# Seven expert halves and a down product at other places of a hand-written scan order, and one value product ahead of a gate-network product

## The chip, the cores and the metric

One Trainium2 chip, one of its cores. The metric is the time of one execution on the device in microseconds (us), the median over repeated runs; lower is better. The core's engines work through separate instruction queues, each strictly in the order in which the kernel issues on it, and meet only through semaphores: TensorE (PE, its weight loads PEld), VectorE (DVE), ScalarE (ACT), GpSimd (POOL), and SyncE (SP), which issues most DMAs.

## What is computed

A layer of gated delta-rule attention, followed by a mixture of eight expert networks with the best two of eight per token, on 8 sequences of 256 tokens of width 128, all in float32. Cut to what matters:

```python
x = x + attention(layernorm(x))       # delta rule, 4 heads of 32, chunks of 32 tokens
x = x + experts(layernorm(x))

# attention: per sequence and head, a serial loop over 8 chunks
def step(S, inp):
    qi, ki, ui, wi = inp
    attn = jnp.where(tri_s, 0.0, qi @ jnp.swapaxes(ki, -1, -2))
    u_i = ui - wi @ S
    o = qi @ S + attn @ u_i
    S = S + jnp.swapaxes(ki, -1, -2) @ u_i
    return (S, o)
# four paths (two convolutions, delta, v) are mixed by weights of a small gate network
# that reads mean and variance of each path ("stats")

# experts
gate_scores = jax.nn.softmax(x @ Wg); topk_scores, topk_idx = jax.lax.top_k(gate_scores, 2)
gate  = jnp.einsum('bsh,ehi->bsei', x, W11)
value = jnp.einsum('bsh,ehi->bsei', x, W12)
fused = gate * jax.nn.sigmoid(gate) * value
expert_out = jnp.einsum('bsei,eih->bseh', fused, W2)   # then the weighted sum of two experts
```

## The kernel before

The 8 sequences are worked as four pairs of 512 tokens. One software pipeline runs over the pairs: a call of `body(u, t, b, c)` projects and normalises pair u, runs the delta rule's serial chunk loop for pair t, the experts for pair b and what is left of the experts of pair c. Five calls cover everything: b is none, 0, 1, 2, 3. The last (`ALONE`) has only experts. In the first there are none. So the serial loop and the experts stand side by side in three calls. Here they are called **scan 1, 2 and 3** (experts of pair 0, 1 and 2) and **tail 1, 2 and 3** (what follows each scan in the same call). Scan 3 has no pair u left: no scores, no masks, no beta.

All experts are computed for all tokens. An expert has 256 inner columns in two **halves** i (half i belongs to expert i // 2), and a half is four steps: `gate` (PE, three matmuls of 128x512: high part, low part of the weights, low part of the input), `sig` (ACT, silu of the gate product into `sg`, in the trace `toep_room`), `value` (PE, three such matmuls), `fuse` (DVE, their product into `fu`, in the trace `v_room`). `y` is the down product of an expert (PE, L585) and needs both its halves; `add` (DVE, four instructions, L1197) weights it by the router and adds it up. `weigh` (DVE, 20 instructions, L1150 to L1175) computes those weights, and `add` needs it; `y` does not.

The chunk loop has eight chunks n. PE computes **u(n)** into ps4, ACT copies it to `u_sb` (L945), PE computes **s(n)** into ps3 and o(n) into ps2 (L441), ACT copies s to `s_sb` (L953), and u(n+1) needs that copy. Between these fixed links stand the lists of `SCAN`: `SCAN[2n]` behind u(n), `SCAN[2n+1]` behind s(n) and o(n). Each engine runs only its own steps of a list, in the list's order:

```python
run(SCAN[2 * n])          # L723 on PE, L947 on ACT
...                       # s(n), o(n)
run(SCAN[2 * n + 1])      # L742 on PE, L955 on ACT
```

On DVE the lists simply follow one another. Other steps that the text names: `norms` (DVE, and behind it the pow on POOL, L362), `norm` (DVE, normalised keys and queries, L1048 to L1057; it sets `kq_ready`), `g` 0 and 1 (PE, scores, ps0 and ps1, need `kq_ready`), `mask` (DVE, L1065 to L1075, needs both g and sets `attn_ready`), `centre` (DVE, L1229 to L1232), `square` (ACT, L850), `spread` (DVE), `stats` (DVE, transposes the statistics), `hidden_s` (PE, L614, the gate network's product over the statistics, needs `stats_ready`), `hidden_x` (PE, L606), `router` (PE, DVE, and an exp on ACT, which loads another activation table, L917), `beta`/`tanh`/`beta_hc` (PE, ACT, DVE).

PSUM banks: gate products go to ps5 and value products to ps6 while a single bank is used for each (`bank_of` gives 0), so a gate product waits for the `sig` of the half before, and a value product for the `fuse` of the half before. Where `two_banks` is true, odd halves use ps0 and ps1, which the scores leave free only once `attn_ready` is set. For pairs 2 and 3 two banks are used throughout.

Of the kernel before, what the change touches and what calls it, by code (L numbers as in the profile page):

```python
# [28 lines left out]
E, FF = 8, 256  # L29
FC = FF // P  # L30
# [26 lines left out]
def dgv(i):  # L57
    return [(what, i) for what in ("dgate", "dsig", "dvalue")]
# [6 lines left out]
         ("dfuse", 13)]  # L65
SCAN = [[("ln_cen", 1), ("ln_sq", 1), ("dy", 6), *dgv(14), ("dadd", 6), ("ln_var", 1), ("conv", 3)],
        [("dfuse", 14), *dgv(15), ("ln_out", 1), ("dfuse", 15)], [("x2t", 1), ("dy", 7), ("dadd", 7)],
        [("q_silu", 0), ("q_hc", 0), ("qk_sq", 0), ("norms", 0)],
        [("router", 1), ("beta", 0), ("tanh", 0), ("beta_hc", 0), ("dstore", 0)],
        [("gate", 0), ("sig", 0), ("value", 0), ("fuse", 0)],  # L70
        [("gate", 1), ("sig", 1), ("value", 1), ("fuse", 1), ("norm", 0), ("gate", 2)],
        [("sig", 2), ("value", 2), ("gate", 3), ("fuse", 2)], [("g", 0), ("weigh", 0)], [("g", 1), ("mask", 0)],
        [("sig", 3), ("value", 3), ("fuse", 3), ("centre", 0), ("square", 0)],
        [("y", 0), ("add", 0), ("centre", 3), ("spread", 0)], [("gate", 4), ("sig", 4), ("value", 4), ("fuse", 4)],
        [("gate", 5), ("square", 3), ("sig", 5), ("value", 5), ("spread", 3)], [("fuse", 5)],
        [("gate", 6), ("centre", 1), ("sig", 6), ("value", 6), ("square", 1)]]
TAIL = [("delta", 0), ("fuse", 6), ("centre", 2), ("spread", 1), ("square", 2), ("y", 1), ("gate", 7), ("sig", 7),
        ("value", 7), ("hidden_x", 0), ("spread", 2), ("fuse", 7), ("stats", 0), ("gate", 8), ("sig", 8),
        ("gelu_set", 0), ("hidden_s", 0), ("add", 1), ("value", 8), ("y", 2), ("gelu", 0), ("exp_set", 0), ("fuse", 8),
        ("logits", 0), ("add", 2), ("y", 3), ("gate", 9), ("exp_in", 0), ("exp", 0), ("sig", 9), ("value", 9),  # L80
        ("softmax", 0), ("fuse", 9), ("add", 3)]

# [21 lines left out]
def build(nc, x, early, taps_row, late, toep_in, w11, w12, w2, out):  # L104
    ctx = ExitStack()
    with ctx:
        def sb(name, *shape):
            return ctx.enter_context(nc.sbuf_tensor(name, [P, *shape], F32))
# [306 lines left out]

        def two_banks(p, i):

            return p >= 2 or 4 <= i < (10, E * FC)[p]

        def bank_of(p, i):  # L420
            return i % 2 if two_banks(p, i) else 0
# [14 lines left out]
        def _(pe):  # L436
# [112 lines left out]
            def body(u, t, b, c):  # L549
# [905 lines left out]
```

## Time and profile before

| | us |
|---|---|
| median of 3 runs | 429.35 |
| lowest and highest | 425.93, 431.18 |
| the profiled execution, whole | 426.13 |
| its span, first to last instruction | 424.4 |
| PE busy | 344.0 |
| DVE busy | 276.2 |
| ACT busy | 146.2 |
| POOL busy | 90.2 |

The profiled execution lies 3.2 us below the median; 1.7 us of it lie outside of its span. The mean granted clock of TensorE in it is 0.918 of full speed. A busy time is no path: the engines wait for one another in turn, and what ends a wait has to be looked up in the timeline.

### The profile page before, as it was taken

To read this page: it belongs to the slowest core of one execution; us is meant where nothing else is said; L and a number is where in the kernel's file an instruction comes from. 1 tells how busy PE (TensorE), PEld (TensorE's weight loads), DVE (VectorE), ACT (ScalarE), POOL (GpSimd) and SP (SyncE) were. 2 spreads that over 40 slices of the span, in tenths; PEclk is the share of its full clock that TensorE was granted. 3 is DMA by queue.
4 is the path that set the end of the run, shared out by engine and by line. 5 is a ranking of instruction groups with operands and counts; after the bars stand their busy time and mean duration, and the time that the engine had idled before them with its cause. 6 is when DMAs were issued, how large, how long until landed. Compare 5 with 4: busy or idle time off the path is not lost.

```text
span 424.4 us, 14279 instructions
## 1 busy us (share of the span) xinstructions
PE 344.0 (81%) x6364; PEld 253.7 (60%) x6364; DVE 276.2 (65%) x639; ACT 146.2 (34%) x264; POOL 90.2 (21%) x152
## 2 busy tenths in 40 slices
PE   7988977954657796888988869899897987867996
PEld 6344963643324565655776557477675755755885
DVE  3788931268747569767755797498739659667554
ACT  1342613301434351453413413533252353133221
POOL 4862000051622061440200715202000000200000
PEclk9699888968598779999999899899989899899999
DMA  7331350005120001110000011200000000000000
GB/s 255 124 94 29 40 123 19 5 3 129 15 37 4 3 2 28 15 25 14 5 2 2 26 29 15 38 3 3 2 28 4 2 0 0 2 25 2 0 2 25
DMA packets 42652, 12.47 MB, mean 29 GB/s; under 512 B 35424, under 2 KB 41696, under 8 KB 42464
## 3 DMA queue, kind: packets, MB, share of 16 engines
q1 hardware_dynamic: 39440, 9.47, 10.4%
q10 hardware_dynamic: 3152, 2.10, 1.6%
q8 instruction: 50, 0.82, 0.8%
q14 instruction: 10, 0.08, 0.1%
HBM read 8.68 MB, written 2.88 MB: 27 GB/s over the span
## 4 chain that ended last, share of the span: by engine, by line
PE 53%; DVE 24%; issue 8%; DMA 6%; ACT 4%; POOL 4%; SPq 0%; DVEq 0%; ACTq 0%
PE ps L546 17%; PE ps L585 12%; PE ps L441 9%; PE ps L485 7%; PE ps L471 3%; DVE x L1197 2%; DVE v_room L1186 2%; PE ps L614 2%; DMA a_d<-a_hc 2%; DMA t<-t_d 1%; DMA t_d<-t_it 1%; POOL t_it L386 1%; DVE toep_room L1230 1%; PE ps L633 1%; POOL rn L362 1%
## 5 line engine op out<-in xcount | busy, mean ns | idle before, releaser
L1186 DVE TENSOR_TENSOR v_room<-toep_room,ps 128x512 f32<-128x512 f32 x64 | 43.7, 684 | 44.1 <-PE ps L546 20.2
L585 PE MATMUL ps<-w_sb,v_room 128*128 128x128 f32 x512 | 64.9, 281 | 8.9 <-DVE x L1197 4.5
L585 PEld LDWEIGHTS ps<-w_sb,v_room 128*128 128x128 f32 x512 | 62.4, 195 | 14.3 <-issue 8.2
L546 PE MATMUL ps<-x_hi,w_sb 128*128 128x512 f32 x128 | 61.7, 482 | 4.0 <-DVE v_room L1186 2.6
L830 ACT ACTIVATE toep_room<-ps 128x512 f32<-128x512 f32 x64 | 38.1, 597 | 60.1 <-PE ps L546 56.6
L546 PE MATMUL ps<-x_lo,w_sb 128*128 128x512 f32 x128 | 52.4, 409 | 0.0
L546 PE MATMUL ps<-x_hi,w_lo 128*128 128x512 f32 x128 | 52.3, 409 | 0.0
L1197 DVE SCALAR_TENSOR_TENSOR x<-ps,rs,x 128x128 f32<-128x128 f32 x128 | 35.8, 342 | 16.5 <-PE ps L585 16.5
L362 POOL TENSOR_TENSOR rn<-ss,mh 128x16 f32<-128x16 f32 x8 | 23.1, 2901 | 65.1 <-DVE ss L1037 65.1
L396 POOL TENSOR_TENSOR g<-gm,mh 128x16 f32<-128x16 f32 x4 | 11.6, 2909 | 112.2 <-DVE gm L1298 112.2
L546 PEld LDWEIGHTS ps<-x_hi,w_sb 128*128 128x128 f32 x128 | 25.3, 198 | 13.3 <-DVE v_room L1186 3.6
L546 PEld LDWEIGHTS ps<-x_hi,w_lo 128*128 128x128 f32 x128 | 25.7, 201 | 5.4 <-issue 2.2
L546 PEld LDWEIGHTS ps<-x_lo,w_sb 128*128 128x128 f32 x128 | 25.1, 196 | 6.0
L441 PEld LDWEIGHTS ps<-u_sb,taps_room 32*32 32x32 f32 x960 | 17.2, 115 | 14.2 <-issue 14.0
L441 PE MATMUL ps<-v_hc,toep_room 32*32 32x64 f32 x768 | 23.8, 281 | 1.5 <-DVE v_hc L1012 1.5
L441 PE MATMUL ps<-u_sb,taps_room 32*32 32x32 f32 x960 | 20.6, 203 | 4.8 <-issue 4.2
L441 PEld LDWEIGHTS ps<-v_hc,toep_room 32*32 32x32 f32 x768 | 20.5, 123 | 3.8 <-DVE v_hc L1012 2.3
L485 PE MATMUL ps<-xnp,wkc 128*128 128x512 f32 x32 | 19.8, 758 | 1.7 <-DVE v_room L1186 1.0
L441 PE MATMUL ps<-vb,t_t 32*32 32x32 f32 x512 | 13.0, 200 | 9.4 <-ACT s_sb L953 9.4
L441 PEld LDWEIGHTS ps<-vb,t_t 32*32 32x32 f32 x512 | 10.0, 110 | 17.0 <-issue 16.4
L850 ACT ACTIVATE psq<-toep_room 128x512 f32<-128x512 f32 x16 | 10.0, 626 | 28.1 <-DVE toep_room L1230 28.1
L945 ACT ACTIVATE u_sb<-ps 128x64 f32<-128x64 f32 x32 | 7.2, 225 | 33.9 <-PE ps L441 33.9
(199 smaller groups left out, 595.7 us busy)
## 6 DMA issues: line engine op xcount, KB each, us to landing
toep_room<-in_toep SPq DMA_DIRECT2D x1, 1536.0 KB, 12.1
a_d<-a_hc SPq DMA_DIRECT2D x4, 256.0 KB, 3.6
t<-t_d SPq DMA_DIRECT2D x4, 256.0 KB, 3.0
v_room<-in_w SPq DMA_DIRECT2D x1, 1024.0 KB, 6.4
v_room<-in_w ACTq DMA_DIRECT2D x1, 1024.0 KB, 6.6
out_y<-x ACTq DMA_DIRECT2D x4, 256.0 KB, 2.3
taps_room<-in_taps SPq DMA_DIRECT2D x1, 768.0 KB, 5.7
x_sb<-in_x SPq DMA_DIRECT2D x1, 768.0 KB, 8.9
```

Source lines behind the costliest of these rows:

```text
L362: pool.tensor_tensor(rn[:, a, :], ss[:, a, :], mh[:, 0:M], ALU.pow).then_inc(s["rn_ready"], 1)
L396: pool.tensor_tensor(g1[:, :], gm[:, :], mh[:, 0:M], ALU.pow).then_inc(s["orn_ready"], 1)
L441: ins = pe.matmul(bank[q, col:col + n], lhs(q), rhs(q), skip_group_check=True, **kw)
L471: ins = pe.matmul(ps[4 + i][:, :], wvc[:, k, :], xnp[:, 2 * i:2 * i + 2, k:k + L], start=(k == 0), stop=(k == 3))
L485: ins = pe.matmul(ps[bank][:, :], w[:, k, :], xnp[:, bass.ds(u * 2, 2), k:k + L], start=(k == 0), stop=(k == 3))
L546: ins = pe.matmul(bank[:, :], a[cols].bitcast(F32R), c[:, :].bitcast(F32R), start=(k == 0), stop=(k == 2))
L585: ins = pe.matmul(yb[:, P * j:P * j + P], fu[:, e % 2, f, P * j:P * j + P], w2_sb[:, FC * e + f, :], start=(f == 0), stop=(f == FC - 1))
L614: pe.matmul(ps[2 + k][:, :], w1s[:, P * k:P * k + P], stats_t[:, :, :].rearrange("p m t -> p (m t)"), start=False, stop=True).then_inc(s[" ...
L830: act.activation(sg[:, i % 2, :], ps[GATE[bank_of(p, i)]][:, :], ACT.Silu).then_inc(s["sg_ready"], 1)
L850: act.activation(psq[:, p, :, :], pcen[:, p, :, :], ACT.Square).then_inc(s["psq_ready"], 1)
L1186: dve.tensor_tensor(fu[:, e % 2, f, :], sg[:, i % 2, :], ps[VALUE[bank_of(p, i)]][:, :], ALU.mult).then_inc(s["fu_ready"], 1)
L1197: ins = dve.scalar_tensor_tensor(x1[:, j, :], ps[out_bank(p, e)][:, P * j:P * j + P], rs[:, j, e:e + 1], x1[:, j, :], ALU.mult, ALU.add)
```

## The change

The steps of the first halves are moved forward in the scan, and one value product in the tail; no instruction is added or removed. In the scan, the first half starts behind s(1) and the router's product comes behind it; halves 0 to 4 and the down product of expert 0 are issued on PE before the second score product's list ends, where halves 0 to 2 and the gate of half 3 stood before. The list `SCAN[12]` is left without steps. With half 4 ahead of the masks, its gate product stays in ps5 and no longer waits for `attn_ready`; half 5 does now. `add` 0, `weigh`, `mask` and the centre and square steps keep their order among each other.

```diff
-        [("q_silu", 0), ("q_hc", 0), ("qk_sq", 0), ("norms", 0)],
-        [("router", 1), ("beta", 0), ("tanh", 0), ("beta_hc", 0), ("dstore", 0)],
-        [("gate", 0), ("sig", 0), ("value", 0), ("fuse", 0)],
-        [("gate", 1), ("sig", 1), ("value", 1), ("fuse", 1), ("norm", 0), ("gate", 2)],
-        [("sig", 2), ("value", 2), ("gate", 3), ("fuse", 2)], [("g", 0), ("weigh", 0)], [("g", 1), ("mask", 0)],
-        [("sig", 3), ("value", 3), ("fuse", 3), ("centre", 0), ("square", 0)],
-        [("y", 0), ("add", 0), ("centre", 3), ("spread", 0)], [("gate", 4), ("sig", 4), ("value", 4), ("fuse", 4)],
+        [("q_silu", 0), ("gate", 0), ("q_hc", 0), ("qk_sq", 0), ("value", 0), ("sig", 0), ("norms", 0)],
+        [("router", 1), ("gate", 1), ("fuse", 0), ("beta", 0), ("tanh", 0), ("beta_hc", 0), ("dstore", 0)],
+        [("sig", 1), ("value", 1), ("gate", 2), ("fuse", 1), ("sig", 2)],
+        [("value", 2), ("fuse", 2), ("norm", 0), ("gate", 3), ("sig", 3)],
+        [("y", 0), ("value", 3)], [("g", 0), ("gate", 4), ("fuse", 3), ("sig", 4), ("weigh", 0)],
+        [("g", 1), ("value", 4), ("mask", 0)], [("fuse", 4), ("centre", 0), ("square", 0)],
+        [("add", 0), ("centre", 3), ("spread", 0)], [],
...
-            return p >= 2 or 4 <= i < (10, E * FC)[p]
+            return p >= 2 or 5 <= i < (10, E * FC)[p]
```

In `TAIL`, `("value", 8)` now stands ahead of `("hidden_s", 0)`; before, it stood behind `("add", 1)`.

PE in scan 1, around the fifth and sixth link of the chunk loop. ps4 is u, ps3 is s, ps5 and ps6 are gate and value products, ps7 is the down product. Before, from u(6) backwards to o(5) and on to half 4:

```order
L441 MATMUL ps2<-u_sb,taps_room 32x32 x4
L585 MATMUL ps7<-w2_sb,v_room 128x128 x8
L441 MATMUL ps4<-vb,t32_t 32x32 x4
L441 MATMUL ps4<-s_sb,wneg_t 32x32 x4
L441 MATMUL ps4<-vb,t32_t 32x32 x4
L441 MATMUL ps4<-s_sb,wneg_t 32x32 x4
L546 MATMUL ps5<-x2_hi,w11_sb 128x512
L546 MATMUL ps5<-x2_hi,w11_lo 128x512
L546 MATMUL ps5<-x2_lo,w11_sb 128x512
L546 MATMUL ps6<-x2_hi,w12_sb 128x512
L546 MATMUL ps6<-x2_hi,w12_lo 128x512
L546 MATMUL ps6<-x2_lo,w12_sb 128x512
```

Now, from the same o(5) to s(6) and o(6):

```order
L441 MATMUL ps2<-u_sb,taps_room 32x32 x4
L441 MATMUL ps4<-vb,t32_t 32x32 x4
L441 MATMUL ps4<-s_sb,wneg_t 32x32 x4
L441 MATMUL ps4<-vb,t32_t 32x32 x4
L441 MATMUL ps4<-s_sb,wneg_t 32x32 x4
L441 MATMUL ps3<-u_sb,taps_room 32x32 x8
L441 MATMUL ps2<-s_sb,taps_room 32x32 x4
L441 MATMUL ps2<-u_sb,taps_room 32x32 x4
L441 MATMUL ps2<-s_sb,taps_room 32x32 x4
L441 MATMUL ps2<-u_sb,taps_room 32x32 x4
```

The down product in front of u(6) and the six matmuls of half 4 behind it stand further up now, so that o(5), u(6) and s(6) follow each other with nothing between.

ACT in scan 1, from the silu of the queries to the link u(3). Before:

```order
L785 ACTIVATE qf<-ps0 128x512
L789 ACTIVATE qk_sq<-qk_hc 128x1024
L945 ACTIVATE u_sb<-ps4 128x64
L917 ACT_TABLE_LOAD
L917 ACTIVATE rt<-rs 128x32
L798 ACTIVATE tb<-ps1 128x512
L953 ACTIVATE s_sb<-ps3 128x64
L830 ACT_TABLE_LOAD
L830 ACTIVATE toep_room<-ps5 128x512
L945 ACTIVATE u_sb<-ps4 128x64
```

Now:

```order
L785 ACTIVATE qf<-ps0 128x512
L789 ACTIVATE qk_sq<-qk_hc 128x1024
L830 ACTIVATE toep_room<-ps5 128x512
L945 ACTIVATE u_sb<-ps4 128x64
L917 ACT_TABLE_LOAD
L917 ACTIVATE rt<-rs 128x32
L798 ACTIVATE tb<-ps1 128x512
L953 ACTIVATE s_sb<-ps3 128x64
L830 ACT_TABLE_LOAD
L830 ACTIVATE toep_room<-ps5 128x512 x2
L945 ACTIVATE u_sb<-ps4 128x64
```

The silu of half 0 has moved ahead of the two table loads, and behind them stand two silus, of halves 1 and 2, ahead of the copy of u(3).

PE in tail 1, from the gate product of half 8 to the down product. Before:

```order
L546 MATMUL ps5<-x2_lo,w11_sb 128x512
L614 MATMUL ps2<-stats_t,late_sb 128x512
L614 MATMUL ps3<-stats_t,late_sb 128x512
L546 MATMUL ps6<-x2_hi,w12_sb 128x512
L546 MATMUL ps6<-x2_hi,w12_lo 128x512
L546 MATMUL ps6<-x2_lo,w12_sb 128x512
L585 MATMUL ps7<-w2_sb,v_room 128x128 x8
```

Now:

```order
L546 MATMUL ps5<-x2_lo,w11_sb 128x512
L546 MATMUL ps6<-x2_hi,w12_sb 128x512
L546 MATMUL ps6<-x2_hi,w12_lo 128x512
L546 MATMUL ps6<-x2_lo,w12_sb 128x512
L614 MATMUL ps2<-stats_t,late_sb 128x512
L614 MATMUL ps3<-stats_t,late_sb 128x512
L585 MATMUL ps7<-w2_sb,v_room 128x128 x8
```

The three matmuls of value product 8 have passed the two of `hidden_s`, which wait for the statistics.

## Rows read from the trace of the kernel before

**Rows 1.** The page's engine shares and the shares of its chain

```profile
PE 344.0 (81%) x6364; PEld 253.7 (60%) x6364; DVE 276.2 (65%) x639; ACT 146.2 (34%) x264; POOL 90.2 (21%) x152
...
PE 53%; DVE 24%; issue 8%; DMA 6%; ACT 4%; POOL 4%; SPq 0%; DVEq 0%; ACTq 0%
```

**Rows 2.** PE's waits over the span: who was waited for, us, times, longest

```profile
PE ps L441 <- ACT s_sb L953: 9.4, 10, 2.3
...
PE ps L614 <- DVE stats_t L1244: 5.6, 4, 1.9
```

**Rows 3.** PE's timeline, scan 2: start, length, work, idle time before and its end

```profile
237.60 0.50 PE L546 MATMUL ps<-x_hi,w_sb 128*128 128x512 f32 x1 [1.36 <-ACT toep_room L830]
...
250.83 2.05 PE L585 MATMUL ps<-w_sb,v_room 128*128 128x128 f32 x16
254.41 0.23 PE L441 MATMUL ps<-vb,t_t 32*32 32x32 f32 x5 [1.53 <-ACT s_sb L953]
...
254.79 0.50 PE L546 MATMUL ps<-x_hi,w_sb 128*128 128x512 f32 x1
...
256.39 0.33 PE L441 MATMUL ps<-u_sb,taps_room 32*32 32x32 f32 x16
...
258.53 0.26 PE L441 MATMUL ps<-vb,t_t 32*32 32x32 f32 x8
...
259.43 0.23 PE L441 MATMUL ps<-s_sb,taps_room 32*32 32x32 f32 x5 [0.45 <-ACT u_sb L945]
...
261.32 1.95 PE L585 MATMUL ps<-w_sb,v_room 128*128 128x128 f32 x16
263.02 0.47 PE L546 MATMUL ps<-x_hi,w_sb 128*128 128x512 f32 x1
```

**Rows 4.** DVE's timeline, scan 2

```profile
240.21 0.69 DVE L1048 TENSOR_TENSOR kn_next<-qk_hc,rn 128x512 f32<-128x512 f32 x1
...
244.41 0.18 DVE L1150 TENSOR_REDUCE st<-rt 128x4 f32<-128x32 f32 x1
...
249.18 0.88 DVE L1065 TENSOR_TENSOR a_hc<-ps,nbm 128x256 f32<-128x256 f32 x2
...
251.49 0.68 DVE L1186 TENSOR_TENSOR v_room<-toep_room,ps 128x512 f32<-128x512 f32 x1
```

**Rows 5.** ACT's timeline, scan 2

```profile
235.66 1.28 ACT L830 ACT_TABLE_LOAD   x1
...
254.06 0.21 ACT L953 ACTIVATE s_sb<-ps 128x64 f32<-128x64 f32 x1
```

**Rows 6.** PE's timeline, scan 1, u(6) and y 1

```profile
170.97 0.23 PE L441 MATMUL ps<-vb,t_t 32*32 32x32 f32 x5 [2.26 <-ACT s_sb L953]
...
177.88 1.95 PE L585 MATMUL ps<-w_sb,v_room 128*128 128x128 f32 x16
```

**Rows 7.** PE's timeline, scan 3, u(6) and y 1

```profile
326.12 0.23 PE L441 MATMUL ps<-vb,t_t 32*32 32x32 f32 x5 [1.91 <-ACT s_sb L953]
...
334.51 1.95 PE L585 MATMUL ps<-w_sb,v_room 128*128 128x128 f32 x16
```

**Rows 8.** PE's timeline, tail 1

```profile
185.35 1.98 PE L614 MATMUL ps<-stats_t,late_sb 128*128 128x512 f32 x4 [1.70 <-DVE stats_t L1244]
...
187.87 1.95 PE L585 MATMUL ps<-w_sb,v_room 128*128 128x128 f32 x16
```

**Rows 9.** PE's timeline, tail 2

```profile
268.96 3.19 PE L614 MATMUL ps<-stats_t,late_sb 128*128 128x512 f32 x4 [1.89 <-DVE stats_t L1244]
...
273.14 1.95 PE L585 MATMUL ps<-w_sb,v_room 128*128 128x128 f32 x16
```

**Rows 10.** Stretches: length, busy time and count of each engine, PE's granted clock, DMA

```profile
327.40:330.90 3.50, 3.50 (x56) 2.45 (x55) 2.33 (x6) 1.34 (x3) 0.00 (x0) 0.53 0.02 5
166.60:178.00 11.40, 8.70 (x195) 6.93 (x184) 10.40 (x24) 3.74 (x10) 4.02 (x9) 1.00 0.28 37
```

**Rows 11.** PE's timeline at the last large wait

```profile
387.01 0.50 PE L546 MATMUL ps<-x_hi,w_sb 128*128 128x512 f32 x1 [2.62 <-DVE v_room L1186]
```

More of the change, by code:

```diff
@@ L78 @@
         ("value", 7), ("hidden_x", 0), ("spread", 2), ("fuse", 7), ("stats", 0), ("gate", 8), ("sig", 8),
-        ("gelu_set", 0), ("hidden_s", 0), ("add", 1), ("value", 8), ("y", 2), ("gelu", 0), ("exp_set", 0), ("fuse", 8),
+        ("gelu_set", 0), ("value", 8), ("hidden_s", 0), ("add", 1), ("y", 2), ("gelu", 0), ("exp_set", 0), ("fuse", 8),
         ("logits", 0), ("add", 2), ("y", 3), ("gate", 9), ("exp_in", 0), ("exp", 0), ("sig", 9), ("value", 9),
```

## The prediction

> **What bounds the kernel now.** I read the page's shares first. PE is busy for 81% of the span and carries 53% of the chain that ended last, DVE 24%, ACT 4% [rows 1]. So neither engine is the bound all the time: stretches in which PE is full alternate with stretches in which it waits for DVE. The waits of PE say where. Ten waits for the copy of s by ACT, L953, make 9.4 us, and four for the statistics, L614, make 5.6 us [rows 2]. Those two kinds are what the change touches.
>
> The first kind is read in scan 2. u(6) on PE starts at 254.41 after 1.53 us idle, released by `s_sb` [rows 3]. The copy itself is short. It starts on ACT at 254.06 [rows 5], because ACT issues `square` 0 ahead of it, and that waits for `centre` 0 on DVE. DVE has no gap there: `norm` from 240.21, `weigh` from 244.41, `mask` from 249.18, `fuse` and `centre` from 251.49 [rows 4]. **So DVE's serial run from `norm` to `centre` 0 sets u(6)**, and PE's products ahead of it only have to be done by then. Behind u(6) PE is the bound until the down product y 1: 6.91 us in scan 2 (254.41 to 261.32) [rows 3] and 6.91 us in scan 1 (170.97 to 177.88) [rows 6]. In scan 3 the same work took 8.39 us (326.12 to 334.51) [rows 7], since TensorE's granted clock was 0.53 in the 3.5 us from 327.40, mostly its lower level of 1.2 GHz, against 1.00 throughout 166.6 to 178 [rows 10]. One fall of the clock there costs 8.39 - 6.91 = **1.48 us**.
>
> y 1 matters: the `fuse` of half 6 needs its buffer back, and delta's `centre`, `square`, `spread`, then `stats` follow on DVE. So a shift of y 1 passes to the whole tail.
>
> **The change part by part.** The number of instructions is equal. I go through what moves.
>
> *When u(6) comes.* The moved work does not leave DVE: between `norm` and `centre` 0 stood two `fuse`, `weigh` and `mask` (fuse 2, fuse 3), and there now stand two as well (fuse 3, fuse 4). What shifts is the start of this run.
>
> - Scan 1: `norm` now follows `fuse` 2 instead of `fuse` 1, so one gate product, one silu and one value product more are ahead of it: 0.7 + 0.6 + 0.7 = **+2.0 us**. A product is 0.7 because six matmuls and the hand-over took 1.60 (254.79 to 256.39) [rows 3]. If the products still ran at 1.2 GHz it would be 2.6 + 0.6 = 3.2; if the earlier start of half 0 is won back in full, 0.
> - Scan 2: before, PE stood 1.36 us in front of gate 1 for a silu [rows 3], which stood behind the 1.28 us table load at 235.66 [rows 5]. In the new order gate 2 waits for the silu of half 1, behind the same load. The gate product of half 1 now stands ahead of `beta` and delays `tanh` and so that load; I estimate gate 2 at 238.1, 0.5 us later than gate 1 was. Behind it come its own 0.7, u(3) 0.3, value product 2 at 0.7 and `fuse` 2 at 0.7 with hand-over, and `norm` starts near 240.6 instead of 240.21: **+0.4 us** (0 to +1.0).
> - Scan 3 has no `norm`; `weigh` follows `fuse` 3 instead of `fuse` 2, one more DVE product of 0.6 (0.68 long in [rows 4]): **+0.6 us** (0 to +0.7).
>
> *From u(6) to y 1.* Half 4, 1.60 us, stood there and covered the round trip by ACT: u(6) to s(6) took 1.98 us (254.41 to 256.39). Uncovered it takes 0.90 as from u(7) to s(7) (258.53 to 259.43, with 0.45 us idle for `u_sb`) [rows 3]. Gain 1.98 - 0.90 = 1.08, so 6.91 becomes 5.83 at full clock. y 0 ran inside the wait and costs 1.7 (261.32 to 263.02) [rows 3]; it leaves no gain, the wait only grows.
>
> *The clock.* Between the end of o(5) and u(6) PE now has nothing at all. In scan 2 y 0 stood from 250.83 and the wait was 1.53 [rows 3]; without y 0 and half 4 in reach the empty time is about 254.4 + 0.4 - 250.8 = 4.0 us, and only 0.9 us of small work and waiting follow before half 5. The trace shows no such wait in a scan. After 1.91 us idle in scan 3 the clock fell, after the 2.26 us of scan 1 it did not (1.00 in [rows 10], which holds that wait), nor after 2.62 us at 387.01, whose matmuls then start 0.34 us apart as at full speed [rows 11]. So a fall is not certain after 2 us; at 4 us I take one in each scan, at 1.48. The bounds are 0 and twice that, if half 5 and half 6 both run wholly at 1.2 GHz. The Trainium skill ("TensorE: Matmul & The Clock Gate", section "Loop structure matters more than you think") says that "whether your matmuls stay warm is determined by your loop nest" and shows a wait between matmuls as the bad case. This rule speaks against the change; by it the fall comes in every scan, as I take it; by the two rows without a fall it would come in none.
>
> Per scan, y 1 then moves by: scan 1 +2.0 - 1.08 + 1.48 = +2.4; scan 2 +0.4 - 1.08 + 1.48 = +0.8; scan 3, whose fall is in its 8.39 already, +0.6 + 5.83 + 1.48 - 8.39 = -0.5. **Scans together: +2.7 us.**
>
> *The tail.* `hidden_s` waited 1.70 us in tail 1 and 1.89 in tail 2 [rows 8, 9]. Value product 8, 0.7 us, now runs within this wait, its PSUM bank being free. From `hidden_s` to y 2 it was 187.87 - 185.35 = 2.52 us [rows 8]; two products over the statistics without the value product are 1.4 to 1.8 of it, so 0.7 to 1.1 goes, I take 0.9. y 2, fuse 8, `add` 2 and y 3 follow each other, and half 9 behind them, so the gain lasts to the end of the tail: 3 x 0.9 = **-2.7 us**. If the statistics themselves came earlier, nothing would be under the value product and its cost back at 0.7; the order on DVE gives no reason for it.
>
> In tail 2 the clock fell behind the wait: 273.14 - 268.96 = 4.18 us for what took 2.52 in tail 1 [rows 8, 9], 1.66 more. With the wait cut to 1.2 us this may be spared. I count half: **-0.8 us**.
>
> At nothing I cost three things. GpSimd's pow starts at the same time, since `norms` keeps its place on DVE. The output store on ACT comes in the same list as before. The masks' 2 us delay in scan 1 delays SyncE's chain of DMAs for the next pair, whose result is first read behind the tail; if that slack were gone, up to 2.0 us would be added, and PE would show a wait for the load of `t16`.
>
> **Sum:** +2.7 - 2.7 - 0.8 = -0.8 us. The profiled execution took 426.13, so 425.3 for one like it. The median shown is 429.35, 3.2 above it; the same step on the median gives **428.5 us**.
>
> **The rivals.**
>
> *A. The clock stays up.* For it: 2.26 and 2.62 us idle without a fall [rows 10, 11]. Then the scans give +2.0 - 1.08, +0.4 - 1.08 and +0.6 + 5.83 - 8.39, together -1.8; the tails up to -3.2, the tail's own fall -1.7: -6.7, **422.7 us**. Against it: a 4 us hole.
>
> *B. Slower: half 5 and half 6 run wholly at 1.2 GHz in all scans.* Place: the products behind s(6). Price: 2.96 instead of 1.48 per scan, +4.4; with tails at -0.7 each and no fall spared, 4.4 + 2.7 - 2.1 = +5.0, **434.4 us**. It decides as soon as the falls cost more than 1.48 + 0.8 / 3 = 1.75 us each: from there the kernel is slower than before. For it: the hole is twice any in the scans before. Against it: PE came back within 3.5 us in scan 3 [rows 10], and part of the low time lies on waits that cost nothing.
>
> *C. DVE's run isn't later at all, since half 0 two steps ahead wins scan 1 back.* Then -0.8 - 2.0 = -2.8, **426.5 us**. For it: PE has work sooner where only the router stood. Against it: the silu behind the table load stops PE either way.
>
> *D. The issue order moves something that I did not see.* Over 2% either way.
>
> **How the numbers follow.** Chances: forecast 0.42, A 0.17, B 0.18, C 0.17, D 0.06. A's and B's ends reach to 422.7 and 434.4; I leave out the last bit of B and take 422 to 434, which also holds the scatter of the runs shown (425.93 to 431.18), since it is as large as the terms. 2%, about what a measurement of this kernel can tell from no change, is 8.6 us. None of A to C reaches it, so faster and slower get only D's share and a little of A and B: 0.04 each; within 2%: 0.92.
>
> **What would show it.** In the changed profile: u(6) in scan 2 preceded by some 4 us idle on PE with `s_sb` as releaser, and DVE without a gap from `norm` to `centre` 0; s(6) 0.9 us behind u(6); a granted clock near 0.5 in the 3 us behind it; u(6) to y 1 7.3 us (5.8 if A). `hidden_s` still waits, about 1.0 to 1.2 us, with y 2 1.4 to 1.8 us behind its start. What would make the prediction wrong: idle time of PE in front of u(6) under 2.5 us, a DVE that stands idle within its run, or falls of the clock at other places than these, which two executions can differ by.

## The result, and the profile after

The changed kernel takes 434.98 us (median of 4 runs: 431.94, 434.5, 435.46, 439.89), the kernel before 427.64 beside it (4 runs, 424.03 to 431.18): **a ratio of 1.0174 [1.0104, 1.0244], slower by 1.0 to 2.4%**. Whether that is more than the 2% which the prediction took as its mark stays open. Predicted were 428.5 and a range to 434, so both are missed; of the rivals B, the slower one, lies nearest (434.4). The profiled execution is the slowest of the four, with a span of 438.1 us and a granted clock of 0.878. Here and below a ratio compares the runs of each kernel within 1.5% of its fastest, a median takes all, so the two differ by about 1% where one run lies far below the others. (The title above says seven expert halves; the scan moves five, halves 0 to 4.)

The page of the kernel after: engine shares and the shares of its chain, which answer to [rows 1].

```profile
PE 354.8 (81%) x6364; PEld 263.7 (60%) x6364; DVE 275.1 (63%) x639; ACT 146.9 (34%) x264; POOL 89.6 (20%) x152
...
PE 54%; DVE 22%; issue 9%; DMA 5%; ACT 5%; POOL 4%; SPq 0%; DVEq 0%; ACTq 0%
```

PE does the same 6364 matmuls and is busy 10.8 us longer: the same work at a lower clock. DVE's time is about the same. PE's waits, to be held against [rows 2] (us in all, times, longest):

```profile
PE ps L441 <- ACT s_sb L953: 15.2, 5, 4.5
...
PE ps L614 <- DVE stats_t L1244: 3.7, 4, 1.1
```

The wait for s, 9.4 us before, is 15.2; the wait for the statistics fell from 5.6 to 3.7, as meant. PE's timeline holds u(6) and y 1 of scans 1, 2 and 3 (against [rows 6, 3, 7]) and, in between, tail 1 (against [rows 8]):

```profile
180.15 0.33 PE L441 MATMUL ps<-vb,t_t 32*32 32x32 f32 x8 [4.44 <-ACT s_sb L953]
...
187.39 1.95 PE L585 MATMUL ps<-w_sb,v_room 128*128 128x128 f32 x16
...
194.81 1.98 PE L614 MATMUL ps<-stats_t,late_sb 128*128 128x512 f32 x4 [0.96 <-DVE stats_t L1244]
196.63 1.95 PE L585 MATMUL ps<-w_sb,v_room 128*128 128x128 f32 x16
...
265.67 0.33 PE L441 MATMUL ps<-vb,t_t 32*32 32x32 f32 x8 [4.53 <-ACT s_sb L953]
...
268.56 0.63 PE L546 MATMUL ps<-x_lo,w_sb 128*128 128x512 f32 x1
...
274.79 2.72 PE L585 MATMUL ps<-w_sb,v_room 128*128 128x128 f32 x16
...
339.13 0.41 PE L441 MATMUL ps<-vb,t_t 32*32 32x32 f32 x6 [4.25 <-ACT s_sb L953]
...
346.96 1.95 PE L585 MATMUL ps<-w_sb,v_room 128*128 128x128 f32 x16
```

The hole of some 4.0 us that was foreseen is there in every scan: 4.44, 4.53, 4.25 us. From u(6) to y 1 it then takes 7.24, 9.12 and 7.83 us, where 5.83 was the full-clock figure. The product at 268.56 shows 0.63 us, and the next one starts 0.43 behind it; at full clock they start 0.23 apart. Stretches through the hole of scan 1 (columns as in [rows 10]):

```profile
174.00:176.00 2.00, 1.22 (x81) 0.92 (x80) 1.76 (x8) 0.22 (x1) 0.00 (x0) 1.00 0.00 0
176.00:178.00 2.00, 0.00 (x0) 0.00 (x0) 1.97 (x5) 0.00 (x0) 1.27 (x1) 0.85 0.80 126
178.00:180.00 2.00, 0.00 (x0) 0.00 (x0) 1.97 (x6) 0.74 (x2) 0.00 (x0) 0.50 0.03 5
180.00:182.00 2.00, 1.43 (x80) 1.30 (x80) 1.97 (x6) 0.22 (x2) 0.00 (x0) 0.50 0.71 72
182.00:184.00 2.00, 2.00 (x12) 1.60 (x6) 1.39 (x4) 1.04 (x3) 0.19 (x1) 0.50 0.03 2
184.00:186.00 2.00, 1.55 (x68) 1.04 (x66) 1.11 (x2) 0.52 (x2) 1.61 (x6) 0.94 0.03 8
```

PE does nothing from 176 to 180. The clock falls to 0.50, its level of 1.2 GHz, while PE is idle, and stays there through u(6), s(6) and half 5, until shortly after 184.

To compare scans across executions I count from the last thing that every version does alike, the copy of `x2t` on ACT (L912) shortly ahead of the first half. In scan 1 of the kernel after it is this row, and 145.19 before:

```profile
149.98 0.60 ACT L912 ACTIVATE x2t<-ps 128x512 f32<-128x512 f32 x1 [2.49 <-PE ps L678]
```

So 4.8 of the 13.7 us between the two profiled spans have arisen before any moved instruction has run: they are scatter between executions (over all the twenty traces the row stands between 143.36 and 151.01). The scans and tails account for the next 6.9, as follows (us; in each cell scan or tail 1, 2, 3; the last line ends at the third table load behind y 1, L830):

| | before | after | difference | predicted |
|---|---|---|---|---|
| copy to u(6) | 25.78, 27.37, 21.34 | 30.17, 29.46, 22.82 | +4.39, +2.09, +1.48 | +2.0, +0.4, +0.6 |
| u(6) to y 1 | 6.91, 6.91, 8.39 | 7.24, 9.12, 7.83 | +0.33, +2.21, -0.56 | +0.40, +0.40, -1.08 |
| y 1 to the table load in the tail | 15.59, 17.43, 15.44 | 14.85, 15.79, 14.74 | -0.74, -1.64, -0.70 | -0.9, -1.7, -0.9 |

The lines add up to +7.96, +1.98 and -3.08, against +3.0, -0.3 and -3.5. (In tail 2 the last cell holds 0.8 for the clock.) The first line is the big miss. DVE's timeline shows where part of it lies, first in scan 2, then in scan 3:

```profile
253.34 0.65 DVE L1057 TENSOR_TENSOR kb<-kn_next,beta 128x512 f32<-128x512 f32 x1
255.06 0.69 DVE L1186 TENSOR_TENSOR v_room<-toep_room,ps 128x512 f32<-128x512 f32 x1 [1.07 <-issue]
...
330.81 0.69 DVE L1186 TENSOR_TENSOR v_room<-toep_room,ps 128x512 f32<-128x512 f32 x1 [3.24 <-PE ps L546]
331.42 0.18 DVE L1150 TENSOR_REDUCE st<-rt 128x4 f32<-128x32 f32 x1
```

DVE's run from `norm` to `centre` 0 has a hole now: `fuse` 3 stands idle for 1.07 us in scan 2 and for 3.24 in scan 3, and `weigh` (L1150) stands behind it. [Rows 4] have no such gap; in scan 3 before, `fuse` 2 waited 1.46 us in that place. Both times value product 3 comes late on PE. In scan 3 y 0 stands ahead of it, which is tested below. In scan 2 it is the clock: the last matmul of value product 3 starts at 254.57, and ahead of it TensorE's granted clock had fallen. The kernel after, and below it the same stretch in e0, a second profile of the same kernel:

```profile
250.21:252.21 2.00, 2.00 (x52) 1.29 (x51) 1.97 (x4) 0.64 (x2) 0.49 (x1) 0.50 0.00 0
```

```profile
250.04:252.04 2.00, 2.00 (x61) 1.91 (x61) 1.97 (x4) 0.82 (x2) 0.50 (x1) 1.00 0.00 0
```

In e0, at 1.00, `fuse` 3 doesn't wait, and u(6) of scan 2 comes 28.22 us behind the copy instead of 29.46.

### The profile page after: what moved, and what is told of

Same layout as the page of the kernel before. It is cut to its first block, busy times and chain, and to the rows that moved or that the text cites. A ratio compares the mean times of both kernels' runs of the same rounds, so it can differ in the third digit from the quotient of the medians.

```text
span 438.1 us, 14278 instructions
## 1 busy us (share of the span) xinstructions
PE 354.8 (81%) x6364; PEld 263.7 (60%) x6364; DVE 275.1 (63%) x639; ACT 146.9 (34%) x264; POOL 89.6 (20%) x152
## 4 chain that ended last, share of the span: by engine, by line
PE 54%; DVE 22%; issue 9%; DMA 5%; ACT 5%; POOL 4%; SPq 0%; DVEq 0%; ACTq 0%
PE ps L546 16%; PE ps L585 13%; PE ps L441 10%; PE ps L485 7%; PE ps L471 3%; DVE x L1197 3%; DVE v_room L1186 2%; DMA a_d<-a_hc 2%; DMA t<-t_d 1%; PE ps L614 1%; DMA t_d<-t_it 1%; ACT L830 1%; PE ps L687 1%; PE ps L633 1%; POOL t_it L386 1%
## 5 line engine op out<-in xcount | busy, mean ns | idle before, releaser
L585 PE MATMUL ps<-w_sb,v_room 128*128 128x128 f32 x512 | 67.1, 287 | 9.1 <-DVE x L1197 4.7
L585 PEld LDWEIGHTS ps<-w_sb,v_room 128*128 128x128 f32 x512 | 64.5, 201 | 15.8 <-issue 10.0
L546 PE MATMUL ps<-x_hi,w_sb 128*128 128x512 f32 x128 | 62.7, 489 | 4.8 <-ACT toep_room L830 3.1
L830 ACT ACTIVATE toep_room<-ps 128x512 f32<-128x512 f32 x64 | 38.0, 596 | 69.4 <-PE ps L546 67.5
L546 PE MATMUL ps<-x_hi,w_lo 128*128 128x512 f32 x128 | 54.8, 428 | 0.0
L546 PE MATMUL ps<-x_lo,w_sb 128*128 128x512 f32 x128 | 54.3, 424 | 0.0
L546 PEld LDWEIGHTS ps<-x_hi,w_sb 128*128 128x128 f32 x128 | 26.5, 207 | 12.9 <-ACT toep_room L830 4.1
L546 PEld LDWEIGHTS ps<-x_lo,w_sb 128*128 128x128 f32 x128 | 26.6, 208 | 6.6
L546 PEld LDWEIGHTS ps<-x_hi,w_lo 128*128 128x128 f32 x128 | 26.8, 210 | 4.7 <-issue 1.2
L441 PE MATMUL ps<-vb,t_t 32*32 32x32 f32 x512 | 13.9, 208 | 15.2 <-ACT s_sb L953 15.2
```

What stands on the lines that cost most here:

```text
L441: ins = pe.matmul(bank[q, col:col + n], lhs(q), rhs(q), skip_group_check=True, **kw)
L546: ins = pe.matmul(bank[:, :], a[cols].bitcast(F32R), c[:, :].bitcast(F32R), start=(k == 0), stop=(k == 2))
L585: ins = pe.matmul(yb[:, P * j:P * j + P], fu[:, e % 2, f, P * j:P * j + P], w2_sb[:, FC * e + f, :], start=(f == 0), stop=(f == FC - 1))
L830: act.activation(sg[:, i % 2, :], ps[GATE[bank_of(p, i)]][:, :], ACT.Silu).then_inc(s["sg_ready"], 1)
```

## The experiments

My theory after the result had two parts: the hole lets TensorE's clock fall, and that costs the time; and u(6) is late because of what now stands ahead of DVE's run. The rival for the first part: the order alone costs the time and the clock is a symptom. For the second part: only the later place of `norm` does it, or only the front (half 0 and gate 1 ahead of the router). The kernel before had medians of 428.57, 428.18, 428.18, 427.5 and 430.1 us in the five groups. All results, each ratio with its 95% interval:

| label | what it is | us, median | ratio to before |
|---|---|---|---|
| e0_after_again | the change | 432.15 | 1.0191 [1.0008, 1.0374] |
| e1_tail_only | before, tail edit alone | 423.61 | 0.9894 [0.9829, 0.9959] |
| e16_tail_again | the same | 423.78 | 0.9909 [0.9865, 0.9953] |
| e2_scan_only | the change without tail edit | 434.63 | 1.0109 [1.0016, 1.0203] |
| e3_hole_filled | the change, hole filled | 427.98 | 0.9933 [0.988, 0.9987] |
| e4_hole_work_back | the change, y 0 and half 4 back | 427.53 | 1.0035 [0.9931, 1.0139] |
| e9_y0_back | the change, only y 0 back | 432.72 | 1.0206 [1.0019, 1.0393] |
| e5_front_only | before, front alone | 427.29 | 0.9925 [0.9878, 0.9972] |
| e6_front_back | the change, front undone | 435.66 | 1.0179 [1.0113, 1.0244] |
| e7_norm_early | the change, `norm` early | 432.51 | 1.0149 [1.0068, 1.0229] |
| e11_filled_norm_early | e7, hole filled | 428.39 | 0.9912 [0.9851, 0.9974] |
| e14_value3_first | the change, value 3 ahead of y 0 | 432.84 | 1.0146 [1.0021, 1.0271] |
| e13_value3_first_filled | e14, hole filled | 426.85 | 0.9972 [0.9888, 1.0055] |
| e18_both | e7 and e14 together | 432.5 | 1.0019 [0.9975, 1.0064] |
| e17_both_filled | e18, hole filled | 426.76 | 0.9882 [0.9793, 0.997] |
| e8_front_and_tail | before, front and tail edit | 422.02 | 0.9947 [0.9908, 0.9986] |
| e15_front_tail_again | the same | 422.9 | 1.001 [0.9932, 1.0087] |
| e12_front_tail_filled | e8, hole filled | 424.41 | 0.9913 [0.9877, 0.995] |

### The two halves of the change, and the change again

e2 is the kernel after with `("value", 8)` of `TAIL` back behind `("add", 1)`; e1 and e16 are the kernel before with it moved ahead of `hidden_s`, and nothing else.

```diff
-        ("gelu_set", 0), ("hidden_s", 0), ("add", 1), ("value", 8), ("y", 2),
+        ("gelu_set", 0), ("value", 8), ("hidden_s", 0), ("add", 1), ("y", 2),
```

> The kernel before with one edit: value product 8 ahead of hidden_s in the tail. My tail term says 2.1 to 3.2 us less than before, ratio near 0.994, with the wait in front of the first L614 of each tail down from 1.7 us to about 1.0 and y 2 about 0.7 to 1.1 us sooner. The rival, that a later wait takes this back (the exp and its table load on ACT), gives a ratio of 1.000 with the interval around it.

> The changed kernel with value product 8 back behind hidden_s, so the scan edit alone. The tail edit alone took 0.7 us off each tail; without it the loss is 2 us larger than the changed kernel's, ratio 1.020 to 1.026. Should the tail edit be worth nothing beside the scan edit, it is 1.017 as with it.

> The changed kernel once more, beside the others on the same chip. Theory H (the clock falls in the empty hole ahead of u(6)) and theory L (late links) both expect the first result again, ratio 1.010 to 1.024; u(6) to y 1 between 7.2 and 9.2 us in each scan.

> The same kernel as tail alone, in five rounds. Three tails at 0.7 us are 2.1 us, ratio 0.995; its first ratio of 0.989 would be 4.5 us, more than its tails can give, so I expect it to come back at 0.993 to 0.997.

The tail edit alone gives 0.9894 and 0.9909, the scan edits alone 1.0109, the whole 1.0174 and again 1.0191. So the two have opposite signs, and the scan is where the change loses. They don't add up well: 1.020 to 1.026 was expected of e2, and by its interval and those of the whole the shares aren't known to better than 1%. PE in tail 1 of e1:

```profile
186.09 1.98 PE L614 MATMUL ps<-stats_t,late_sb 128*128 128x512 f32 x4 [1.01 <-DVE stats_t L1244]
187.91 1.95 PE L585 MATMUL ps<-w_sb,v_room 128*128 128x128 f32 x16
```

From `hidden_s` to y 2 it takes 1.82 us, 2.52 before [rows 8]: 0.70 won, with 1.01 us of the wait left. Tail 2 wins 2.35, since its clock doesn't fall now; in e5, which lacks the edit, it didn't fall either (2.52 us behind a wait of 1.86), so that part isn't sure to be the edit's. The tails of e1 together win 3.7 us; its median and that of e16, 5.0 and 3.7 us below the kernel before's of the same groups, are in line with that (2.1 to 3.2 was expected).

### Filling the hole

e3 is the kernel after with five products more on PE in the hole. They compute gate product 4 again into ps5, once the silu has read it, and nobody reads them.

```diff
+                def fill(_):
+                    if b is not None:
+                        pe.wait_ge(s["sg_ready"], b * E * FC + 5)
+                        for _i in range(5):
+                            expert_product(ps[5], w11_sb, w11_lo, 4)
...
-        [("add", 0), ("centre", 3), ("spread", 0)], [],
+        [("fill", 0), ("add", 0), ("centre", 3), ("spread", 0)], [],
```

> The changed kernel, and in each of the three scans 15 matmuls of 128x512 more on PE behind o(5), in front of u(6). They compute the gate product of half 4 again into ps5 and nobody reads it; they take 15 x 0.234 = 3.5 us of a hole of 4.3 to 4.5 us. Theory H (the empty hole lets the clock fall, and half 5 and half 6 pay): the time falls by 4 to 5 us from the changed kernel's 435, ratio to before near 1.006, and the stretch from u(6) to y 1 takes 5.8 to 6.0 us in all three scans instead of 7.2, 9.1 and 7.8. Theory L (all comes from links that are issued or released late ahead of the hole): no change, ratio 1.017, as u(6) waits for DVE either way.

PE of e3, u(6) and y 1 of scan 1 (what stands behind L585 in the kernel is 7 lines further there):

```profile
176.90 0.39 PE L546 MATMUL ps<-x_lo,w_sb 128*128 128x512 f32 x1
178.09 0.23 PE L441 MATMUL ps<-vb,t_t 32*32 32x32 f32 x5 [0.81 <-ACT s_sb L960]
...
183.90 1.95 PE L585 MATMUL ps<-w_sb,v_room 128*128 128x128 f32 x16
```

PE works to within 0.81 us of u(6), which comes no sooner: 31.55, 29.47 and 22.79 us behind the copy. But u(6) to y 1 is 5.81, 5.82 and 5.81 us, the 5.83 that was worked out for full clock. That is 6.75 us less than in the kernel after over three scans, and the median is 427.98. **Fifteen useless matmuls in each scan make the changed kernel 1 to 2% faster** (from 434.98, or 432.15 in e0, to 427.98; the ratios, from 1.0174 or 1.0191 to 0.9933, say 2.4 to 2.5%). The instructions behind u(6) and their order are the same, so for the time from u(6) to y 1 the clock is the cause and not a symptom. The filled kernel is about as fast as the kernel before (428.57 in the same group; 1.006 was expected of it): without the falls the late u(6) still takes what the tail and the shorter way from u(6) to y 1 give.

### Putting real work back

e4 moves y 0 and half 4 back to where they stood (half 4 with its second bank); e9 moves only y 0.

```diff
# e4 (e9: only the moves of y 0)
-        [("y", 0), ("value", 3)], [("g", 0), ("gate", 4), ("fuse", 3), ("sig", 4), ("weigh", 0)],
-        [("g", 1), ("value", 4), ("mask", 0)], [("fuse", 4), ("centre", 0), ("square", 0)],
-        [("add", 0), ("centre", 3), ("spread", 0)], [],
+        [("value", 3)], [("g", 0), ("fuse", 3), ("weigh", 0)],
+        [("g", 1), ("mask", 0)], [("centre", 0), ("square", 0)],
+        [("y", 0), ("add", 0), ("centre", 3), ("spread", 0)], [("gate", 4), ("sig", 4), ("value", 4), ("fuse", 4)],
```

> The changed kernel with y 0 put back in front of u(6) and half 4 back behind it; the front, the place of norm behind fuse 2 and the tail edit stay. Theory H: the wait ahead of u(6) is 2.5 us or less and the clock stays up in most scans, u(6) to y 1 takes 6.9 us as before the change, and with the gains of front and tail the ratio is 0.985 to 0.995. Theory L (norm late by one product pair): u(6) still comes late, ratio near 1.005.

> The changed kernel with only the down product y 0 back in front of u(6): 1.8 us of the 4.4 us hole are worked, 2.6 us stay idle, and nothing stands between u(6) and s(6). Theory H with a clock that outlasts such a wait, as it did twice in the profile before (2.26 and 2.62 us): u(6) to y 1 takes 5.8 us and the ratio is 0.975 to 0.990, the best yet. If 2.6 us of idle time plus the 0.9 us of round trip behind u(6) are enough for a fall, it takes 7.2 to 9 us and the ratio is 1.000 to 1.010, between the changed kernel and the filled one. Theory L: 1.015.

e4 is no slower than the kernel before that can be told (1.0035), but 0.985 to 0.995 was expected of it, since it keeps the tail edit. Its u(6) of scan 1 still comes late (30.64 us behind the copy), and behind a wait of 2.48 us there the clock fell (8.36 us from u(6) to y 1). e9 is as slow as the change (1.0206). PE in scan 2 of e9:

```profile
253.97 2.05 PE L585 MATMUL ps<-w_sb,v_room 128*128 128x128 f32 x16
259.09 0.23 PE L441 MATMUL ps<-vb,t_t 32*32 32x32 f32 x5 [3.07 <-ACT s_sb L953]
...
261.83 0.63 PE L546 MATMUL ps<-x_hi,w_sb 128*128 128x512 f32 x1
...
266.21 1.95 PE L585 MATMUL ps<-w_sb,v_room 128*128 128x128 f32 x16
```

y 0 shortens the hole only to 3.06 us, and the clock falls in all three scans (half 5 at 0.63 us a product; 7.12 to 9.34 from u(6) to y 1). And `fuse` 4 on DVE now waits for y 0 to leave `fu`:

```profile
256.16 0.69 DVE L1186 TENSOR_TENSOR v_room<-toep_room,ps 128x512 f32<-128x512 f32 x1 [1.40 <-PE ps L585]
```

### The front

e5 is the kernel before with half 0 ahead of the router's product and gate 1 ahead of beta's steps, as in the change; e6 is the change without that, and with `norm` behind `fuse` 1 again, as before.

```diff
# e5, against before
-        [("q_silu", 0), ("q_hc", 0), ("qk_sq", 0), ("norms", 0)],
-        [("router", 1), ("beta", 0), ("tanh", 0), ("beta_hc", 0), ("dstore", 0)],
-        [("gate", 0), ("sig", 0), ("value", 0), ("fuse", 0)],
-        [("gate", 1), ("sig", 1), ("value", 1), ("fuse", 1), ("norm", 0), ("gate", 2)],
+        [("q_silu", 0), ("gate", 0), ("q_hc", 0), ("qk_sq", 0), ("value", 0), ("sig", 0), ("norms", 0)],
+        [("router", 1), ("gate", 1), ("fuse", 0), ("beta", 0), ("tanh", 0), ("beta_hc", 0), ("dstore", 0)],
+        [("sig", 1), ("value", 1), ("fuse", 1)],
+        [("norm", 0), ("gate", 2)],
```

> The kernel before with only the front moved: half 0 behind s(1), gate product 1 behind the router and ahead of beta, the rest where it was. Theory L: half 0 waits for the split input and runs ahead of u(2), and gate 1 delays beta, tanh and the table load, so that norm starts later by 1 to 2.5 us in scan 1 and 0.5 to 1 us in scan 2, and u(6) with it: 1.5 to 4 us slower than before, ratio 1.004 to 1.009. Theory H alone: the hole isn't there, y 0 and half 4 stand where they stood, ratio 1.000.

> The changed kernel with the front undone: half 0 and half 1 behind the beta list as before, norm behind fuse 1 as before; y 0, half 3 and half 4 stay where the change put them, ahead of u(5), and the tail edit stays. Theory L: u(6) comes where it came before the change, give or take 1 us, which takes 4 to 7 us off the changed kernel's 435, ratio 1.000 to 1.007. Theory H: the hole remains and the clock falls in it, so most of the loss stays, ratio 1.010 to 1.015.

The front alone isn't slower (0.9925), and without it the change is as slow as with it (1.0179), with u(6) 28.01, 28.97 and 23.04 us behind the copy. So the front isn't the cause. Its price in scan 1 depends on the clock. Half 0 of this front runs at a granted clock of 0.50 in every profile, and the profiles differ in when the clock rises. Here are the 3 us from 5 us behind the copy on, in e8 and below it in e15, which are one and the same kernel:

```profile
149.28:152.28 3.00, 3.00 (x42) 2.81 (x32) 0.72 (x3) 1.74 (x3) 2.96 (x2) 0.50 0.00 0
```

```profile
152.74:155.74 3.00, 3.00 (x49) 2.05 (x38) 0.98 (x3) 1.74 (x3) 2.96 (x2) 0.94 0.00 0
```

In the eleven profiles with this front and 0.50 there, s(2) is copied 11.0 to 11.3 us behind the copy of `x2t`; in the five with 0.88 to 0.99 (e2, e9, e14, e15, e18) at 8.6 to 8.9 (6.54 before). The front alone then costs u(6) of scan 1 2.2 us at the low clock (27.95 in e5, 27.94 in e8) and nothing at the high one (25.76 in e15, 25.78 before). With the high clock u(6) of scan 1 is 2.03 us later than before in e2, as predicted (+2.0).

### What makes u(6) late

```diff
# e7
-        [("value", 2), ("fuse", 2), ("norm", 0), ("gate", 3), ("sig", 3)],
+        [("value", 2), ("norm", 0), ("fuse", 2), ("gate", 3), ("sig", 3)],
# e14
-        [("y", 0), ("value", 3)], [("g", 0), ...
+        [("value", 3), ("y", 0)], [("g", 0), ...
```

e18 has both edits, and e11, e13 and e17 are e7, e14 and e18 with the fill of e3.

> The changed kernel with norm ahead of fuse 2 on DVE. Theory L (the late norm holds up u(6)): norm starts 2 us sooner and u(6) 2 to 4 us sooner in scans 1 and 2, ratio near 1.005. Theory H: u(6) moves by less than 1 us, as fuse 3 waits for value product 3 on PE anyway, and the hole and the fall of the clock stay, ratio 1.012 to 1.020.

> The changed kernel with the hole filled by 15 idle matmuls in each scan and norm ahead of fuse 2 on DVE. u(6) to y 1 stays at 5.8 us. If the late norm matters, 1 to 3 us less than the filled kernel, ratio 0.985 to 0.991; if not, 0.993 as that.

> The changed kernel with value product 3 ahead of y 0 and nothing else. u(6) comes 1 to 1.8 us sooner in scan 3 and up to 1 us in scan 2 if the theory of value product 3 holds; the hole is shorter by as much, some 2.8 to 4 us, and the clock still falls in it, so the ratio is 1.008 to 1.016. If the theory is wrong, u(6) stays and the ratio is 1.017.

> The changed kernel with the hole filled, and value product 3 ahead of y 0. If fuse 3 and with it weigh were held up by value product 3 behind y 0, weigh starts 1.0 to 1.8 us sooner in scans 2 and 3 and s_sb(5) with it, from 29.1 and 22.4 us behind the x2t copy to 28 and 21; less in scan 1, where norm ends late. Ratio 0.985 to 0.993. If DVE's run is held up by something else, these times stay within 0.3 us.

> The same without the filling matmuls. u(6) as in the other; the hole is 2.5 to 3.5 us, the clock falls in it in most scans and u(6) to y 1 takes 7.2 to 9.4 us. Ratio 1.000 to 1.012, 4 to 8 us above the filled one.

> The changed kernel with norm ahead of fuse 2, value product 3 ahead of y 0, and the hole filled with 15 idle matmuls in each scan. If norm and value product 3 hide each other, u(6) comes 1 to 2 us sooner than with either alone: near 28 us behind the x2t copy in scan 1 (26 if the front runs at full clock), 27 in scan 2, and 21 to 22 in scan 3, with u(6) to y 1 at 5.8 us. Ratio 0.980 to 0.990. If u(6) stays at 30 and 28 in scans 1 and 2, a third thing holds it up and the ratio is 0.990 to 0.997.

In e7, `norm` starts earlier (11.76 us behind the copy in scan 2, after 14.46) and u(6) hardly (28.69, after 29.46, e0 28.22), nor does it in scan 1 (30.20, after 30.17): the theory that only `norm` counts fell. DVE in scan 2 of e7:

```profile
241.25 0.68 DVE L1048 TENSOR_TENSOR kn_next<-qk_hc,rn 128x512 f32<-128x512 f32 x1
...
247.56 0.69 DVE L1186 TENSOR_TENSOR v_room<-toep_room,ps 128x512 f32<-128x512 f32 x1 [1.11 <-issue]
```

What was won ahead of `norm` is partly lost as a wait in front of `fuse` 3. e13 takes away what stands ahead of value product 3. DVE in scan 3 of e13, `fuse` 3 and the first instruction of `weigh`:

```profile
320.32 0.69 DVE L1193 TENSOR_TENSOR v_room<-toep_room,ps 128x512 f32<-128x512 f32 x1 [1.45 <-PE ps L546]
320.93 0.18 DVE L1157 TENSOR_REDUCE st<-rt 128x4 f32<-128x32 f32 x1
```

1.45 us where it was 3.24, and the copy of s(5) in scan 3 comes 20.66 us behind the copy of `x2t` instead of 22.44. That part is shown: y 0 ahead of value product 3 costs 1.8 us in scan 3. In scans 1 and 2 it gives nothing that can be told from scatter: 28.23 in scan 2 is 1.2 us sooner than in after and e3, but e0 has 28.22 without the edit. Both edits together don't help scan 2 either (29.87); DVE there in e18:

```profile
244.71 0.68 DVE L1048 TENSOR_TENSOR kn_next<-qk_hc,rn 128x512 f32<-128x512 f32 x1
...
249.24 0.68 DVE L1186 TENSOR_TENSOR v_room<-toep_room,ps 128x512 f32<-128x512 f32 x1
251.71 0.69 DVE L1186 TENSOR_TENSOR v_room<-toep_room,ps 128x512 f32<-128x512 f32 x1 [1.80 <-issue]
```

`fuse` 2 at 249.24 stands behind `norm`. As value products have a single bank in pairs 0 and 1, value product 3 must wait for it, and `fuse` 3 for that: 1.80 us idle. PE's row of value product 3 shows this wait, and a product at the lower clock behind it (0.80 long instead of 0.50):

```profile
249.97 0.80 PE L546 MATMUL ps<-x_hi,w_sb 128*128 128x512 f32 x1 [2.36 <-DVE v_room L1186]
```

In e7 the same wait is 0.37 us. So `norm` ahead of `fuse` 2 gives with one hand and takes with the other; a kernel with a second bank for value product 3 was not run.

All three fills again bring u(6) to y 1 to 5.80 to 5.82 us in every scan, with medians of 428.39, 426.85 and 426.76, against 432.51, 432.84 and 432.5 unfilled: 4.1, 6.0 and 5.7 us. In the unfilled e14 and e18 the clock fell in all six scans, behind holes of 2.41 to 4.28 us. Where the hole has shrunk, the fill is too long: in e17 u(6) of scan 2 waits for it (31.56 us behind the copy, with the copy of s(5) at 29.63). So its ratio came where two causes that hide each other would put it (0.980 to 0.990), but not by their way: u(6) came 30.67, 31.56 and 22.18 us behind the copy and was expected near 28, 27 and 21 to 22.

### A version that keeps what is good

e8 and e15 are e5 with the tail edit; e12 puts two such products behind y 0 there.

> The kernel before with the front moved and the tail edit, y 0 and half 4 where they were and norm behind fuse 1. If the two gains measured alone (0.9925 and 0.9894) add up, the ratio is 0.982, some 421 us; if the front's 0.9925 was scatter, it is 0.989. Each tail should be 0.7 us shorter than before and each scan from u(6) to y 1 6.9 us at full clock.

> The same kernel as front and tail, in five rounds. If both gains are real it beats tail alone in the same call by 1 to 3 us, ratio 0.982 to 0.990; if the front was scatter it equals tail alone.

> Front and tail moved, y 0 and half 4 where they were before the change, and 6 matmuls of 128x512 (1.4 us, a repeat of gate product 3 into ps5 that nobody reads) between y 0 and u(6). In the run without them the clock fell in scans 1 and 3 behind a wait of 1.9 us, u(6) to y 1 took 8.3 and 8.6 us. Theory H: 6.9 us in all scans, 1 to 3 us less than front and tail alone, ratio 0.978 to 0.990. If the falls come from something else, they stay, ratio 0.986 to 0.995.

PE in scan 1 of e8:

```profile
172.22 0.23 PE L441 MATMUL ps<-vb,t_t 32*32 32x32 f32 x5 [1.94 <-ACT s_sb L953]
...
173.41 0.63 PE L546 MATMUL ps<-x_lo,w_sb 128*128 128x512 f32 x1
...
180.53 0.72 PE L585 MATMUL ps<-w_sb,v_room 128*128 128x128 f32 x5
```

The medians, 422.02 (10 runs) and 422.9 (12), stand 1.4% and 1.1% below the kernel before's of the same groups, those of the tail edit alone (423.61, 423.78) 1.2% and 0.9%. The ratios (0.9947 and 1.001, against 0.9894 and 0.9909) order them the other way round. Which is better is not resolved, and the 0.982 that the sum of both gains would be isn't there; both beat the changed kernel (434.98, 432.15) by 2 to 3%. Filling e8's smaller holes (1.94 us in front of u(6)) took the falls of the clock out of its trace (u(6) to y 1 7.74, 6.91 and 6.92 us, after 8.31, 6.91 and 8.61) but nothing off its median (424.41).

## Why the prediction was wrong

**What bounds the kernel: right.** PE is paced by DVE through `s_sb` and `stats_t`, and the two waits are what changed: 9.4 to 15.2 us and 5.6 to 3.7.

**The hole: right.** About 4.0 us idle ahead of u(6) was worked out for scan 2; 4.53 came, and 4.44 and 4.25 in the others.

**The step that failed is "When u(6) comes"**: +3.0 us over three scans, and +7.96 in the profiled execution (e0: +6.9; e2, with the same scan: +4.4). DVE's run was taken to be as long as before, merely shifted. Three things were missed.

- Scan 1: the products of the front ran at 1.2 GHz, for which the text had an end of +3.2 and took +2.0. +4.39 came, +4.59 in e0, and +2.03 where the clock rose earlier (e2).
- Scan 2: `norm` itself came 0.95 us later (e0) and not 0.4. A part of it is the price of a product: the 1.60 us for two in [rows 3] make 0.8 each, and 0.7 was taken. With that alone u(6) came 0.85 later. In the profiled execution the clock fell ahead of value product 3 as well, `fuse` 3 waited 1.07 us within the run, and it was +2.09.
- Scan 3: y 0 had moved ahead of value product 3, which `fuse` 3 and so `weigh` wait for: +1.48 instead of +0.6, and e13 shows the cause.

The prediction named "a DVE that stands idle within its run" as what would make it wrong; it never asked, product by product, when PE delivers what each `fuse` reads, nor at which clock. The kernel before scatters here too: with its scan order u(6) of scan 3 came 21.34 us behind the copy in two profiles and 19.90 in one (e1).

**The price of the clock: mis-sized.** A fall in each scan was taken, and it came in all 24 scans of the eight profiles in which nothing stands between u(6) and s(6) and the hole isn't filled (after, e0, e2, e6, e7, e9, e14, e18). It was priced at 1.48 us. From u(6) to y 1 it took 7.9 us on average in these 24, 5.81 filled: 2.1 us a fall, 6.3 us in all instead of 4.4. That is beyond the 1.75 us from which rival B was to decide. B's picture was near it, not exact: half 5 ran all but wholly at 1.2 GHz, half 6 in scan 2 of the profiled run and in four scans of the others. The rule quoted from the Trainium skill ("TensorE: Matmul & The Clock Gate", section "Loop structure matters more than you think"), that the loop nest decides whether matmuls stay warm, agrees with all 24. The size of 1.48 was read off a single fall, in scan 3 before: there the first four matmuls of half 4 still ran at the high clock, and only the fifth and sixth were slow. Single falls cost 1.3 to 3.6 us.

**From u(6) to y 1: right.** 5.83 us at full clock was predicted; 5.80 to 5.82 in all four filled kernels.

**The tail: right.** 0.9 us a tail was taken, from 0.7 to 1.1; 0.70 to 0.74 came in tails 1 and 3. Half of 1.66 us was counted for tail 2's clock, and 0.9 came in the profiled execution, 1.65 in e1. That 0.8 was right is luck: behind the statistics' wait all 1.66 were spared (1.83 us from `hidden_s` to y 2), and 0.7 was lost at y 1, where the clock was still low from the scan.

**The sum.** With the measured terms it would have been +7.96 + 1.98 - 3.08 = +6.9 us on the profiled pair, beside 7.3 us between the medians. The other 6.8 us between the two profiled spans (4.8 ahead of scan 1, 2.0 elsewhere) are no part of the change that I can show.

**Faster, same, slower.** The 0.92 for "within 2%" holds for the ratio itself, 1.0174, though its interval reaches beyond 2%. What was too narrow is the range: rival B stood at 434.4, and the term for u(6) had an upper end 1.9 us above its value (+1.2, +0.6, +0.1) that was never added to B.

**Open.** Why the clock rises earlier in the front of scan 1 in some executions than in others; why it fell ahead of value product 3 of scan 2 in the profiles of after and e3 and not in that of e0; and where the 6.8 us outside of the scans come from.

## What to carry to other kernels

Work that sits in the shadow of a wait and looks free may be what keeps TensorE's clock up: before you take it out, add the idle time that is left, and price the fall on a stretch that runs at full clock now. When work moves ahead on one engine, list for every reader on the waiting engine when its input now arrives; a shift passed on whole is only the case in which nothing overtook. If a hole can't be closed with work, a few idle products may pay: here fifteen matmuls a scan gave 1 to 2%. Count them by the hole: too many hold up the link that they fill the time for.

## What the runs showed of the hardware

- In one execution the clock was low for a stretch and in another of the same kernel high: 0.50 in e8 and 0.94 in e15 from 5 to 8 us behind the copy of `x2t` in scan 1, with s(2) at 11.3 and 8.7 us; 0.50 in the kernel after and 1.00 in e0 ahead of value product 3 of scan 2.
- With half 4 behind u(6), waits of up to 2.5 us in front of it (before, e1, e4, e5, e8, e15, e16) were followed by a fall in some scans and not in others: 1.90 us and 8.61 from u(6) to y 1 in e8, 2.26 us and 6.91 before. With nothing between u(6) and s(6) a fall followed in all 24 scans, behind 2.41 to 4.53 us.
- The wait in front of u(6) is paid for a second time behind it: 2.1 us on average and 1.3 to 3.6 in single scans, between u(6) and y 1 (7.24 in the kernel after and 9.42 in e2, against 5.81 filled).
- Executions of one kernel spread widely: the kernel before from 418.37 to 433.5 us over all its runs. Ahead of the first moved instruction, where all kernels are alike, the twenty profiles are up to 7.7 us apart. A single profile per kernel would have put that on the change.
